# Rope attention: six of the 32 units of row maxima as a difference of key halves, its positive part by ScalarE

## The reference

```python
def _L0_ffn_ref(src, Wq, Wk_c, Wv_c, Wk, Wv, Wo, ...):
    q = (src @ Wq).reshape(Bb, Tt, H, DH).transpose(0, 2, 1, 3)
    k = (src @ Wk_c @ Wk).reshape(Bb, Tt, H, DH).transpose(0, 2, 1, 3)
    v = (src @ Wv_c @ Wv).reshape(Bb, Tt, H, DH).transpose(0, 2, 1, 3)
    q = _apply_rope(q, sin, cos)
    k = _apply_rope(k, sin, cos)
    attn = jnp.einsum('bhqd,bhkd->bhqk', q, k) / np.sqrt(DH).astype(np.float32)
    attn = jax.nn.softmax(attn, axis=-1)
    sa = jnp.einsum('bhqk,bhkd->bhqd', attn, v)
```

## Time and profile before

| what | value |
|---|---|
| median of three runs | 4140.08 us |
| span of the profiled execution, first to last instruction | 4133.9 us |
| mean granted clock of TensorE | 0.943 |
| TensorE busy | 3634.7 us (88%) |
| VectorE busy | 3108.4 us (75%) |
| ScalarE busy | 2040.9 us (49%) |
| first and second attention stage, maxima to last exponential | 83.9 to about 810 us, 1494.6 to about 2219 us |
| maxima of a ring tile (L877) | 2048 reads, 1309.2 us busy |
| exps (L819) | 1024, 992.0 us busy |

### The profile page before, as it was taken

How to read it: one execution, slowest core, us unless ns; L and a number is a source line. 1 busy time by engine, 2 the same in 40 slices (tenths; PEclk the granted TensorE clock), 3 DMA queues, 4 the chain that set the end, 5 groups by cost and what they waited for, 6 DMA issues and landing times. The chain is left out here.

```text
span 4133.9 us, 60386 instructions
## 1 busy us (share of the span) xinstructions
PE 3634.7 (88%) x20845; PEld 1603.4 (39%) x20845; DVE 3108.4 (75%) x7157; ACT 2040.9 (49%) x3136; POOL 1267.6 (31%) x1378
## 2 busy tenths in 40 slices
PE   6999999989888779999998896647999999999865
PEld 2222222254445422222224445533444444444555
DVE  7999999467566699999993785456777777877444
ACT  2577777631343337777775123323444444444433
POOL 1011011011311201101101123434666676676543
PEclk8899999999999879999999997878999999999887
DMA  4211111220200041111115002322000000000133
GB/s 114 60 53 56 55 56 54 91 66 0 77 1 1 12 110 51 55 56 55 54 47 157 1 11 78 88 61 72 2 2 2 2 7 7 2 10 5 43 99 95
DMA packets 330712, 192.85 MB, mean 47 GB/s; under 512 B 172194, under 2 KB 285626, under 8 KB 330410
## 3 DMA queue, kind: packets, MB, share of 16 engines
q1 hardware_dynamic: 314634, 155.93, 14.1%
q0 software_dynamic: 14048, 32.79, 2.7%
q10 hardware_dynamic: 1728, 0.28, 0.0%
HBM read 119.74 MB, written 67.90 MB: 45 GB/s over the span
## 5 line engine op out<-in xcount | busy, mean ns | idle before, releaser
L877 DVE TENSOR_REDUCE ra_mh<-PS 128x1 f32<-128x512 f32 x2048 | 1309.2, 686 | 55.1 <-PE PS L737 34.7
L819 ACT ACTIVATE ra_p<-PS 128x1024 f32<-128x1024 f32 x1024 | 992.0, 1019 | 310.2 <-PE PS L745 309.8
L754 PE MATMUL PS<-ra_p,ra_va 128*32 128x512 f32 x4096 | 565.6, 606 | 0.3
L745 PE MATMUL PS<-ra_q,ra_k 75*128 75x512 bf16 x2048 | 538.5, 383 | 3.8 <-ACT ra_p L819 1.5
L2703 ACT ACTIVATE ca_p<-PS 128x1024 f32<-128x1024 f32 (+3 forms) x384 | 305.2, 811 | 369.6 <-PE PS L2596 366.2
L2774 POOL TENSOR_TENSOR ca_s<-ca_s,ca_p 128x1024 f32<-128x1024 f32 (+3 forms) x256 | 414.7, 1620 | 65.2 <-ACT ca_p L2703 44.5
L737 PE MATMUL PS<-ra_k,ra_q 48*128 48x512 bf16 x1024 | 408.2, 399 | 17.2 <-DMA ra_qo<-q_parts 16.6
L737 PE MATMUL PS<-ra_ko,ra_qo 48*128 48x512 bf16 x1024 | 409.0, 399 | 9.4 <-DVE ra_mh L877 9.4
L737 PEld LDWEIGHTS PS<-ra_k,ra_q 48*128 48x128 bf16 x1024 | 95.0, 93 | 659.3 <-DVE ra_mh L877 374.6
L2592 PE MATMUL PS<-ca_q,ca_k 64*128 64x512 f32 (+3 forms) x1536 | 318.8, 495 | 0.0
L2613 PE MATMUL PS<-ca_p,ca_v 128*64 128x512 f32 (+3 forms) x1536 | 290.3, 498 | 1.6 <-POOL ca_p L2763 1.6
(11 more groups left out here) (270 smaller groups left out, 5654.5 us busy)
## 6 DMA issues: line engine op xcount, KB each, us to landing
ra_k<-k_parts SPq DMA_DIRECT2D x128, 144.0 KB
ra_q<-q_parts SPq DMA_DIRECT2D x128, 144.0 KB
ao_ot<-o_heads SPq DMA_DIRECT2D x16, 1024.0 KB, 9.0
o_heads<-rp_rot POOLq DMA_DIRECT2D x122, 128.0 KB, 4.2
f_xg<-expert_tokens SPq DMA_DIRECT2D x56, 256.0 KB, 3.5
expert_outputs<-f_yb SPq DMA_DIRECT2D x56, 256.0 KB
expert_tokens<-X SPq DMA_DIRECT2D x28, 256.0 KB
q_parts<-rp_parts SPq DMA_DIRECT2D x48, 128.0 KB
```

The source lines that it names most:

```text
L745: mm = pe.matmul(PS[:, j, :], K[0:KROWS, ub, j, (step % KT) * P:(step % KT + 1) * P], Q[0:KROWS, ub, j, (step // KT) * BT:(step // KT + 1) ...
L754: mm = pe.matmul(PS[VW * j:VW * (j + 1), 4, :], VA[:, ub, step % KT, j, :], PR[:, s % 2, j, :], start=(s % KT == 0), stop=(s % KT == KT - ...
L819: act.activation(PR[:, s % 2, PH * pair:PH * (pair + 1), :], PS[:, PH * pair:PH * (pair + 1), :], ACT.Exp, scale=float(DH) ** -0.5).then_i ...
L877: dve.tensor_reduce(mh[:, pair, KT * odd + t, h:h + 1], PS[:, 5 + number % 3, :], AX.X, ALU.max).then_inc(s_bank[number % 3], 1)
```

## The change

Of three of the eight query tiles (t = 5, 6, 7) the even head's two ring tiles change. The first becomes a *difference*: queries times (keys of the first half minus keys of the second half), one matmul with both key halves stacked in the rows, the second negated. ScalarE writes its positive part to SBUF. The second tile, *larger*, is the plain scores of the second half; VectorE adds the positive part and takes the maximum in one instruction, since max(a, b) = b + max(a − b, 0). Three tiles in each of two pairs are six units an iteration. The number and the order of TensorE's matmuls stay; the query tiles are taken in the order 0, 1, 2, 5, 3, 6, 4, 7, which puts the differences into the first halves of steps 1, 3, 7, 9, 11 and 15. The stacked queries and keys are loaded by eight more DMAs a pair, and GpSimd flips the sign of the second key half (`flip`) ahead of its `split`. Of ScalarE's two negations one remains; GpSimd makes the first bf16 part.

```diff
-    LOADS = PH * 2 + 2
+    LOADS = PH * 2 + 2 + 4 * HALVES
...
+    ORDER, DOUBLED = (0, 1, 2, 5, 3, 6, 4, 7), (5, 6, 7)
+    def tiles_of(pair):
+        tiles = []
+        for t in ORDER:
+            if t in DOUBLED:
+                tiles += [("difference", pair, t), ("tile", pair, t, 0, 1), ("larger", pair, t), ("tile", pair, t, 1, 1)]
+            else:
+                tiles += [("tile", pair, t, h, odd) for h in range(HALVES) for odd in range(PH)]
+        return tiles
...
             def load(n, pair, u):
...
+                for h in range(HALVES):
+                    whole, mid = slice(HD2 // 2 * h, HD2 // 2 * h + KW), slice(HD2 // 2 * h + KW, HD2 // 2 * (h + 1))
+                    sp.dma_start(KD[whole, u, pair, :], bass.AP(k.tensor, k.offset + BT * h, [
+                        [SEQ, KW], [1, BT]])).then_inc(s_qk[pair][u], 16)
+                    sp.dma_start(KD[mid, u, pair, :], bass.AP(k.tensor, k.offset + BT * h, [
+                        [PARTS * SEQ, DH], [1, BT]])).then_inc(s_qk[pair][u], 16)
+                    sp.dma_start(QD[whole, u, pair, DCOLS], bass.AP(q.tensor, q.offset + DCOLS.start, [
+                        [SEQ, DH], [0, PARTS], [1, SEQ - DCOLS.start]])).then_inc(s_qk[pair][u], 16)
+                    sp.dma_start(QD[mid, u, pair, DCOLS], bass.AP(q.tensor, q.offset + DCOLS.start + DH * SEQ, [
+                        [SEQ, DH], [1, SEQ - DCOLS.start]])).then_inc(s_qk[pair][u], 16)
...
             def split(t, pair):
...
+                ch.link(pool.tensor_copy(mp[:, pair, u, 0, :], nm[:, :]))
                 ch.link(pool.tensor_tensor(nr[:, :], nm[:, :], mp[:, pair, u, 0, :], ALU.subtract))
...
+            def flip(n, pair):
+                pool.wait_ge(s_qk[pair][n % 2], 16 * LOADS * (n // 2 + 1))
+                if n:
+                    pool.wait_ge(s_mp, 2 * n + pair - 1)
+                keys = KD[LOW, n % 2, pair, :]
+                pool.tensor_scalar(keys, keys, -1.0, None, ALU.mult).then_inc(s_flip, 1)
...
+                if n + 1 < ITERS:
+                    flip(n + 1, 0)
                 split(n, 1)
...
+                elif use[0] == "difference":
+                    _, pair, t = use
+                    pe.wait_ge(s_flip, 2 * n + pair + 1)
+                    pe.matmul(PS[:, 5 + number % 3, :], QD[:, u, pair, t * P:(t + 1) * P], KD[:, u, pair, :],
+                              start=True, stop=True).then_inc(s_tile, 1)
...
-                act.activation(nm[:, :], rows, ACT.Copy, scale=-1.0).then_inc(s_neg, 1)
-                act.wait_ge(s_neg, passes + 1)
-                act.activation(mp[:, pair, t % 2, 0, :], rows, ACT.Copy, scale=-1.0).then_inc(s_bank[number % 3], 1)
+                act.activation(nm[:, :], rows, ACT.Copy, scale=-1.0).then_inc(s_bank[number % 3], 1)
...
+            def over_zero(number):
+                i = DIFFERENCES.index(number)
+                act.wait_ge(s_tile, number + 1)
+                if i >= 2:
+                    act.wait_ge(*been_read(DIFFERENCES[i - 2] + 2))
+                act.activation(over[:, i % 2, :], PS[:, 5 + number % 3, :], ACT.Relu).then_inc(s_bank[number % 3], 1)
...
                             negate(n + 1, 0)
+                        for use in halves_of(n)[2 * s]:
+                            if use[0] == "difference":
+                                over_zero(len(PRO) + len(RING) * n + ring_of(n).index(use))
                         for pair in range(2):
                             if n or s >= KT * pair:
                                 exps(n, s, pair)
...
+                if use[0] == "larger":
+                    t = use[2]
+                    dve.wait_ge(*been_read(number - 2))
+                    dve.tensor_tensor_reduce(tile, tile, over[:, DIFFERENCES.index(number - 2) % 2, :], 1.0, LOWEST,
+                                             ALU.add, ALU.max, accum_out=mh[:, pair, t, 1:2]).then_inc(s_bank[number % 3], 1)
```

More of the change, by code:

```diff
@@ L588, in rope_attention @@
     mh = sb("ra_mh", [P, 2, PH * KT, HALVES])
+    over = project.ROT[:, :, BT:SEQ]
+    KW, LOW = PARTS * DH, slice(HD2 // 2, HD2)
+    QD = QO[0:HD2, :, :, :]
+    KD = KO[0:HD2, :, :, :].rearrange("p a b s -> p (a b s)")[:, 4 * PARTS * P:4 * PARTS * P + 4 * BT].rearrange(
+        "p (u pair s) -> p u pair s", u=2, pair=2)
+    DCOLS = slice(min(DOUBLED) * P, SEQ)
     m = sb("ra_m", [P, 2, PH * KT])
@@ L600, in rope_attention @@
     s_os = output_rows.s_os
-    s_va, s_tile, s_mx, s_neg, s_mp, s_pv, s_of, s_ch = (
-        sem("ra_" + n) for n in ("v_ready", "tile_ready", "m_ready", "m_negated", "m_parts", "pv_done", "o_free", "chain"))
+    s_low, s_flip = sem("ra_lowest"), sem("ra_keys_flipped")
+    s_va, s_tile, s_mx, s_mp, s_pv, s_of, s_ch = (
+        sem("ra_" + n) for n in ("v_ready", "tile_ready", "m_ready", "m_parts", "pv_done", "o_free", "chain"))
     s_bank = [sem(f"ra_bank_read{i}") for i in range(3)]
@@ L623, in behind @@
         return (u if s >= KT else 1 - u), (s - KT) % STEPS
+    DIFFERENCES = [i for i, use in enumerate(PRO) if use[0] == "difference"]
+    for n in range(ITERS):
+        DIFFERENCES += [len(PRO) + len(RING) * n + i for i, use in enumerate(ring_of(n)) if use[0] == "difference"]
     def store(engine, n, h, pairs=(0, 1)):
@@ L717, in _ @@
                 if n + 1 < ITERS:
+                    flip(n + 1, 1)
                     split(n + 1, 0)
@@ L721, in _, with ring @@
         def _(pe):
-            def ring(number, use, n2, u):
+            def ring(number, use, n2, u, n):
                 if number >= 3:
@@ L729, in ring @@
                     pe.transpose(PS[0:PH * KT, 5 + number % 3, 0:P], m[:, use[1], :], IDN[:, :]).then_inc(s_tile, 1)
-                else:
-                    pair, c = use
-                    t, h, odd = c // (PH * HALVES), c // PH % HALVES, c % PH
+                elif use[0] == "difference":
[3 more added lines that the diff above has]
+                              start=True, stop=True).then_inc(s_tile, 1)
+                else:
+                    pair, t, h, odd = use[1:] if use[0] == "tile" else use[1:] + (1, 0)
                     if odd:
@@ L773, in _ @@
                     pe.wait_ge(s_qk[1][0], 16 * LOADS)
-                ring(i, use, 1, 0)
+                ring(i, use, 1, 0, 0)
             pe.wait_ge(project.s_set, project.SETS)
@@ L844, in _ @@
             act.wait_ge(project.s_rd, 2 * NBLK)
-            negate(0, 0)
-            values(0, 16)
+            for i, use in enumerate(PRO):
+                if use[0] == "difference":
+                    over_zero(i)
+                elif use[0] == "turn":
+                    negate(0, 0)
+                    values(0, 16)
             for it in range(ITERS // 2):
@@ L870, in read @@
             def read(number, use):
-                if use[0] == "turn":
+                if use[0] in ("turn", "difference"):
                     return
-                pair, c = use
-                t, h, odd = c // (PH * HALVES), c // PH % HALVES, c % PH
+                pair, tile = use[1], PS[:, 5 + number % 3, :]
                 dve.wait_ge(s_tile, number + 1)
-                dve.tensor_reduce(mh[:, pair, KT * odd + t, h:h + 1], PS[:, 5 + number % 3, :],
-                                  AX.X, ALU.max).then_inc(s_bank[number % 3], 1)
-                if c == TILES - 1:
+                if use[0] == "larger":
[3 more added lines that the diff above has]
+                                             ALU.add, ALU.max, accum_out=mh[:, pair, t, 1:2]).then_inc(s_bank[number % 3], 1)
+                else:
+                    t, h, odd = use[2:]
+                    dve.tensor_reduce(mh[:, pair, KT * odd + t, h:h + 1], tile,
+                                      AX.X, ALU.max).then_inc(s_bank[number % 3], 1)
+                if use in ENDS:
                     for k in range(3):
```

26 lines of the change are left out of this document (17 added, 9 removed).

## The result

The kernel after took 4287.85 us (median of 4 runs, 4286.16 to 4289.55), the kernel before 4139.92 (4 runs, 4134.70 to 4146.66): a ratio of 1.0358, 95% interval 1.0340 to 1.0376. The forecast was 4287. The profiled execution has a span of 4287.3 us, 153.4 more than before.

The account below looks back on a forecast made before the run. The prediction took TensorE to be the bound. Its terms, +150 (Relu), −12 (turns) and +9 (starts), made +147 us on a span of 4133.9, so 4281, plus 6.2 from span to median: 4287 us, range 4235 to 4345.

Parts of the forecast that it names:

- What bounds the kernel: In the steady part of the first attention stage, TensorE is the bound; VectorE is nearly full but not late.
- The Relu: Ahead of the exps in six of 16 steps, it stalls TensorE 0.84 us each, 178 times: +150 us (+134 to +169).
- The count of TensorE's waits: Sign: L745's second pair of scores starts late with ScalarE as releaser, about 180 times, some 150 us in all.
- VectorE's relief at the turn: At 62 turns, freer VectorE gives back 0.2 of the 0.30 us TensorE waits: −12 us (0 to −19).
- the 4.6 that was named: Sign: an iteration grows by about 4.6 us, 6 x 0.84 less 2 x 0.2.
- The starts: At each stage's start, 16 more SP issues bring first scores about 4.5 us later: +9 us for two (−4 to +20).
- Loads, flip, copy: Longer loads and GpSimd's flip and copy stay hidden: cost 0; far ends +39 for loads, +62 for GpSimd without cover.
- The clock: TensorE's granted clock was expected to stay at 1.00 in the stages despite the new pauses.
- rival 1: ScalarE's idle time in each step hides the Relu: 4117 to 4137 us, not slower; chance 4%.
- rival 2: The pair's longer loads land late, at the far end +39 us: 4326 us; chance 10%.
- rival 3: Stalls make TensorE's clock fall to 0.93 in the stages, +105 us: 4392 us; chance 7%.
- rival 4: The Relu's stall partly falls where TensorE waited anyway; half of it gives 4212 us; chance 7%.

Follow-up runs that it names:

- difference_in_second_half: Kernel after, with difference tiles in second half-steps and the Relu behind both exps: 4139.95 us, ratio 1.0006 to the kernel before.
- the last five experiments: Kernel after with query tiles reordered for fewer VectorE reads beside the turn, the last two also issuing difference loads earlier: 4177.74, 4136.42, 4166.80, 4133.00, 4116.02 us.
- relu_between: Kernel after, with the Relu moved between the step's two exps: 4159.48 us, ratio 1.0046 to the kernel before.
- relu_32_columns: Kernel after, with the Relu still ahead of both exps but covering 32 of 512 columns: 4223.09 us, ratio 1.0201 to the kernel before.
- loads_and_flip_alone: Kernel after, with all tiles plain and read by VectorE; extra loads, flip, moved copy and tile order stay: 4144.34 us, ratio 1.0016 to the kernel before.
- relu_first_plain_loads: Kernel after, without the extra loads and flip, a plain tile standing for the difference, Relu still first: 4292.83 us, ratio 1.0364 to the kernel before.
- turn_between_light_halves: Kernel after, with query tiles 5 and 6 first, their halves in turn, and Relus between or behind the exps: 4166.80 us, ratio 1.0060 to the kernel before.

## Why the prediction was right, and where it was not

*What bounds the kernel.* Right: difference_in_second_half took the work from VectorE and gained nothing.

*The Relu.* Right in each step: Relu at X+1.39 (forecast X+1.39), exps from X+1.88 (1.89), second pair's scores at X+3.87 (3.89), 0.846 us per Relu (0.84). The two stages grew by 71.4 and 74.4 us where 89 Relus were priced at 74.8. The count of TensorE's waits was not the one named: a Relu makes two, one per pair of heads, so 158 in that stretch where 79 Relus stand. The form that it took was the cheaper one, 597 ns; a maximum of the same shape on VectorE took 687, and what costs is where the Relu stands in ScalarE's queue. The Trainium skill, "ScalarE: Activation LUTs", section "Rules for kernel authors", has the rule to keep relu on VectorE, with a factor for bf16. These rows of fp32 tiles out of PSUM do not bear it out, as the forecast held, but no run here has a Relu on VectorE. By form, 140 to 780 us:

```profile
L951 DVE TENSOR_REDUCE ra_mh<-PS 128x1 f32<-128x512 f32 x698 | 456.9, 687 | 80.6 <-PE PS L794 74.4
...
L947 DVE CUSTOM_DVE_ANT_0 PS<-PS,rp_rot 128x512 f32<-128x512 f32 x81 | 56.7, 700 | 47.9 <-PE PS L794 47.9
L901 ACT ACTIVATE rp_rot<-PS 128x512 f32<-128x512 f32 x81 | 48.4, 597 | 113.6 <-PE PS L794 111.8 <-PE PS L786 1.8
L754 POOL TENSOR_SCALAR ra_ko<-ra_ko 32x512 bf16<-32x512 bf16 x27 | 40.1, 1486 | 138.5 <-DMA ra_qo<-q_parts 138.5
...
L947 DVE DVE_READ_ACCUMULATOR2_ANT ra_mh<- 128x1 f32 x81 | 11.5, 142 | 0.0
```

*VectorE's relief at the turn, −12 us: wrong, it was 0.* The step that failed is "After the change VectorE has the stall of step 3 or 11 to fold the maxima, so most of this goes", by which 0.2 of the 0.30 us of a turn were to come back. The maxima were folded in the stall (L957, over at 298.04), and VectorE then stood idle for 0.60 us; but TensorE waits for the reads behind that, the transpose for the second of four, the odd tile for the fourth. So TensorE's idle time at the transpose fell from 0.18 to 0.06 us, and the odd tile came 0.25 behind its partner instead of 0.12 (rows answering to the earlier trace rows):

```profile
297.85 0.19 DVE L957 TENSOR_REDUCE ra_m<-ra_mh 128x16 f32<-128x32 f32 x1
...
298.64 2.61 DVE L951 TENSOR_REDUCE ra_mh<-PS 128x1 f32<-128x512 f32 x4 [0.60 <-PE PS L794]
...
299.99 0.28 PE L782 MATMUL PS<-IDN,ra_m 128*16 128x128 f32 x1
...
300.10 1.03 PE L802 MATMUL PS<-ra_q,ra_k 75*128 75x512 bf16 x4
...
301.06 0.39 PE L794 MATMUL PS<-ra_k,ra_q 48*128 48x512 bf16 x1
...
301.31 0.39 PE L794 MATMUL PS<-ra_ko,ra_qo 48*128 48x512 bf16 x1
```

It is a latency (two reads of 0.69 in line behind one half step's tiles), not a load, and the last five experiments show it part by part. An iteration grew by 5.08 us and not by the 4.6 that was named, for the 2 x 0.2 did not come.

*The starts, +9 us: too much, about +2.* First scores came at 119.50, 4.2 later (4.5 forecast), but those of the second stage only 1.1 later. That 4.2 is so near to 4.5 is in part luck: relu_between, whose program is the same up to there, had its first scores at 117.76, loads_and_flip_alone at 116.71. And the first stage grew by 3.0 less than the second (71.4 and 74.4), because before the change TensorE stayed at its lower clock level longer after the first scores. After the change the granted clock is 0.51 up to 126 us and 1.00 behind it; before, from 126 to 136 us, it was 0.74, a mixture of both levels, which puts the rise at about 131. TensorE had paused 3.22 us ahead of the first scores, with no such pause before; but the pause does not decide it. With one of 3.26 us relu_32_columns was still at the lower level from 126 to 136 us, and without one loads_and_flip_alone was at 1.00 there. In the second stage the rise came 8 us behind the first scores both before and after. So nothing ties the 3.0 us to the change. TensorE's row of the first scores, and busy time by stretch after:

```profile
119.50 1.01 PE L802 MATMUL PS<-ra_q,ra_k 75*128 75x512 bf16 x2 [3.22 <-DMA ra_q<-ra_ko]
```

```profile
119.50:126.00 6.50, 6.14 (x16) 0.86 (x16) 3.17 (x5) 2.54 (x3) 0.00 (x0) 0.51 0.34 110
126.00:136.00 10.00, 9.62 (x41) 2.21 (x39) 9.15 (x18) 4.85 (x6) 2.63 (x5) 1.00 0.02 5
```

The stretch from 126 to 136 us before, in relu_32_columns and in loads_and_flip_alone:

```profile
126.00:136.00 10.00, 9.67 (x35) 1.74 (x33) 7.92 (x14) 3.49 (x5) 1.12 (x3) 0.74 0.00 0
126.00:136.00 10.00, 10.00 (x28) 1.30 (x26) 6.03 (x11) 2.79 (x4) 1.48 (x1) 0.50 0.00 1
126.00:136.00 10.00, 9.62 (x39) 2.12 (x37) 9.40 (x18) 4.36 (x5) 2.87 (x5) 1.00 0.00 1
```

*Loads, flip, copy: 0.* Right for the iterations, by loads_and_flip_alone (42.71 us as before) and relu_first_plain_loads (47.789 us as after). The sizes were off: the extra eight issues took 4.0 us instead of 5.1 (SyncE's issues after, the first and last of a pair's 14, answering to the earlier trace rows), and the flip 1.49 us, near the top of what was given for it. The cover is thin: as soon as an order puts a difference first in a pair's list, TensorE waits for one or the other.

```profile
306.19 0.79 SPq L665 DMA_DIRECT2D ra_k<-k_parts  x1
...
310.16 0.58 SPq L672 DMA_DIRECT2D ra_qo<-q_parts  x1
310.78 0.55 SPq L677 DMA_DIRECT2D ra_ko<-k_parts  x1
...
314.31 0.47 SPq L683 DMA_DIRECT2D ra_qo<-q_parts  x1
```

*The clock.* Right: 1.00 in the steady part, with idle times of 0.2 to 0.4 us before each pair's scores behind six of 16 steps. The Trainium skill, "TensorE: Matmul & The Clock Gate", section "A second HAM failure mode: psum-queue depth-cycling", warns that short pauses can make the clock swing; these did not.

*The rivals.* ScalarE's idle time hides a Relu only if its tile is there in time: rival 1 is the kernel difference_in_second_half, not this one. TensorE never waited for the loads (rival 2) between 140 and 780 us in this order, the clock (rival 3) did not fall, and the stall (rival 4) came in full.

*The sum.* The terms were 150, −12 and +9; they measured 148.8 (twice 74.4), 0 and +2.3, and 2.3 more came behind the second stage, in code that the change does not touch, which was not in the forecast and stays unexplained (in the ten other kernels' profiles that part took 1917.0 to 1926.5 us, so it differs by more than that). That is 153.4 against 147. The 6.2 us between span and median were for the most part the spread of the runs: after the change each run lies 1.8 to 2.3 us above its own span, and the median 0.6 above that of the profiled execution. So that the forecast was within 1 us is luck, for its misses cancelled; its main term is good to 1%. The inner bounds, 4260 to 4320, are narrower than all ends added up (4251 to 4329); the time lies in both.

## What to carry to other kernels

An instruction put into an in-order queue costs by how late its input comes and how long it holds the engine, against the slack of what stands behind it, however idle the engine is on average: before an edit, write down when the input is ready, what queues behind, and by when that is needed. Relief for an engine that the bound does not wait for is worth nothing by its amount; look for the few places where a ring of buffers makes the bound wait for one read, and put the lighter work there. When a stall goes, the next one has its slack already in the trace: here the flip, then the loads, each plain in the waits.

## What the runs showed of the hardware that was not expected

- GpSimd's flip of 32x512 bf16 took 1.49 us every time (1479 to 1510 ns over 64 of them in turn_between_light_halves), 3.5 times the 0.42 us of its subtraction of 16x128 fp32.
- The issue of one of the eight small loads on SyncE took 0.30 to 0.68 us (medians of L677 to L683 in the kernel after), where the pair's six full loads took 0.58 to 0.80 (L665 to L672).
- Add with maximum took 700 ns, 13 more than the plain maximum, and a read of the accumulator, 142 ns, beside it.
- TensorE's granted clock rose to 1.00 at quite different times behind the first scores of the first stage: some 16 us before the change, 6 after it and 19 in relu_32_columns, where TensorE was busy 10.00 of 10 us from 126 to 136 us at 0.50.
